# Linear attention with a mixture of experts on one core: a new beginning, two PSUM banks each for two block tiles, and a table computed in single steps

## The reference, cut to what matters

```python
x = L0_attn_x                                   # 8 x 512 x 128, float32
n = layernorm(x)                                # over the last axis
q, k, v = n @ wq.T + bq, n @ wk.T + bk, n @ wv.T + bv      # 16 heads of 8
out = ((q @ k.T) * causal) @ v                  # per head, no softmax
x = x + out @ wo.T + bo
m = layernorm(x)                                # 4096 tokens
probs = softmax(m @ Wg)                         # 8 experts
topk_p, topk_i = top_k(probs, 2)
for each token and each of its two experts e:
    y = relu(m @ W1[e] + b1[e]) @ W2[e] + b2[e] # 128 -> 256 -> 128
    x = x + topk_p * y
```

## Time and profile before

| what | us |
|---|---|
| median of 3 runs (lowest, highest) | 295.95 (294.81, 296.66) |
| the profiled execution's own time | 294.35 |
| its span in the profile | 292.6 |
| busy: PE, PEld, DVE, ACT, POOL | 242.0, 173.6, 202.1, 170.0, 180.4 |

### The profile page before, as it was taken

One profiled execution on the slowest core, in us unless ns is written; L12 is line 12 of the kernel. 1 busy time (PEld: TensorE's weight loads), 2 busy tenths in 40 slices (PEclk: granted clock), 3 DMA queues, 4 the chain that ended last, 5 costly groups with the idle time before them and its releaser, 6 DMA issues.

```text
span 292.6 us, 6373 instructions
## 1 busy us (share of the span) xinstructions
PE 242.0 (83%) x1392; PEld 173.6 (59%) x1392; DVE 202.1 (69%) x598; ACT 170.0 (58%) x675; POOL 180.4 (62%) x175
## 2 busy tenths in 40 slices
PE   0389999999999999999877196599999999989810
PEld 0134466666666666665566085487777877778600
DVE  4865999888999998999966647733344343333386
ACT  3233348888989888877696154345555555545400
POOL 3055565220877878687727777777767666666730
PEclk9999999999999999999955579979999999999965
DMA  6960000000010111010101451333444333349548
GB/s 198 307 189 0 0 3 0 0 2 2 27 39 30 39 38 38 30 46 28 58 18 55 101 143 57 87 90 112 137 119 106 96 95 92 88 101 365 164 124 262
DMA packets 32431, 25.49 MB, mean 87 GB/s; under 512 B 4337, under 2 KB 30201, under 8 KB 32396
## 3 DMA queue, kind: packets, MB, share of 16 engines
q1 hardware_dynamic: 23824, 14.52, 18.5%
q0 software_dynamic: 4320, 8.47, 8.7%
q10 hardware_dynamic: 4252, 2.10, 2.6%
HBM read 13.92 MB, written 11.61 MB: 87 GB/s over the span
## 4 chain that ended last, share of the span: by engine, by line
PE 71%; DVE 16%; issue 5%; ACT 4%; DMA 1%; ACTq 1%; DVEq 0%
PE ps L961 18%; PE ps L1060 14%; PE ps L1049 13%; PE ps L931 8%; PE ps L1042 3%; PE ps L970 2%; DVE x_sb L917 2%; PE ps L933 2%; PE ps L952 2%; PE ps L981 2%; DVE back L677 2%; DVE x_sb L915 2%; PE ps L973 1%; DVE back L668 1%; DMA bias_bc<-b_o 1%
## 5 line engine op out<-in xcount | busy, mean ns | idle before, releaser
L417 POOL DMA_INDIRECT returned<-y_sb,xt x71 | 70.9, 998 | 28.5 <-issue 25.1
L389 POOL DMA_INDIRECT dispatched<-rows,slot x64 | 65.0, 1016 | 38.0 <-ACT rows L483 16.6
L872 DVE TENSOR_SCALAR y_sb<-ps,xt 128x128 f32<-128x128 f32 x71 | 24.9, 350 | 61.1 <-PE ps L1061 61.1
L961 PE MATMUL ps<-back,causal 128*128 128x512 f32 x128 | 63.4, 618 | 0.4 <-DVE back L668 0.4
L1060 PE MATMUL ps<-w_sb,hT 128*128 x284 | 49.8, 298 | 8.4 <-DVE y_sb L872 6.8
L1049 PE MATMUL ps<-xT,w_of 128*128 128x128 f32 x284 | 49.4, 298 | 2.9 <-ACT hT L565 1.9
L373 POOL TENSOR_TENSOR back<-qkv 128x1024 f32<-128x1024 f32 x16 | 31.3, 1958 | 32.7 <-ACT qkv L504 32.4
L1060 PEld LDWEIGHTS ps<-w_sb,hT 128*128 128x128 f32 x284 | 37.6, 192 | 22.2 <-issue 22.2
L557 ACT ACTIVATE xT<-ps 128x128 f32<-128x128 f32 x71 | 19.7, 278 | 51.1 <-PE ps L1042 49.9
L565 ACT ACTIVATE hT<-ps,b_col 128x128 f32<-128x128 f32 x142 | 44.1, 366 | 1.3 <-PE ps L1049 1.3
L677 DVE TENSOR_TENSOR back<-ps,qkv 128x1024 f32<-128x1024 f32 x32 | 38.9, 1216 | 6.8 <-PE ps L961 6.8
(11 more groups left out here) (168 smaller groups left out, 416.1 us busy)
## 6 DMA issues: line engine op xcount, KB each, us to landing
xt<-dispatched SPq DMA_DIRECT2D x71, 65.0 KB, 1.9
back<-returned SPq DMA_DIRECT2D x7, 512.0 KB, 7.4
x_sb<-x SPq DMA_DIRECT2D x8, 256.0 KB, 5.2
out<-x_sb ACTq DMA_DIRECT2D x7, 256.0 KB, 2.5
returned<-y_sb,xt POOLq DMA_INDIRECT x71, 2.4
w_sb<-w SPq DMA_DIRECT2D x1, 1024.0 KB, 5.7
w_sb<-w SPq DMA_DIRECT2D x2, 512.0 KB, 7.7
dispatched<-rows,slot POOLq DMA_INDIRECT x64, 2.3
```

Of the source, the lines that this page charges most:

```text
L389: pool.indirect_dma_start(out=dispatched[:, :], out_offset=bass.IndirectOffsetOnAxis(ap=slot[:, g * K + k:g * K + k + 1], axis=0), in_=row ...
L417: pool.indirect_dma_start(out=returned[:, :], out_offset=bass.IndirectOffsetOnAxis(ap=xt[:, n % G, D:D + 1].bitcast(I32), axis=0), in_=y_s ...
L872: dve.tensor_scalar(y_sb[:, n % G, :], ps_y, xt[:, n % G, D + 1:D + 2], None, ALU.mult).then_inc(y_done, 1)
L961: mm = pe.matmul(ps_run[g % 2][:, u, :], causal[:, :], outer[:, g % OUTER_RING, 512 * u:512 * (u + 1)], start=True, stop=True)
```

## The change

1. **Biases:** the four biases come as one array, so ACT issues three loads instead of six, and DVE waits for three.
2. **Unread matmuls:** PE no longer waits for the q/k/v weights before everything. It issues nine 128x128 float32 matmuls of the identity with itself as soon as the identity is there, two more behind the first transpose, and two more between the first projection and its bias. Nothing reads them. They write bank 2.
3. **Later logarithms:** the groups are tiles 0 to 3, 4 to 11 and 12 to 31. `deviation1(1)` runs in ACT's slot 0 instead of -2, `deviation1(2)` in slot 7 instead of 1, and DVE's `scale1_out(2)` in its slot 5 instead of 0.
4. **Statistics in DVE's first slots:** ahead of the slots DVE takes the statistics of batches 0 to 3 only, and those of batches 4 to 7 at the end of its slots -1, 0, 1 and 2.
5. **Two banks each:** `ps_x` alternates between banks 2 and 0, `ps_y` between banks 5 and 6. PE's waits are for the block before the last one.
6. **Second table's steps apart:** `rest_table(k)` runs one step, or a few short ones, behind block steps 3, 5, 7, 9, 10, 11, 13, 15 and 17. No operation is dropped.

```diff
-    AHEAD = [range(0, T), range(T, 2 * T), range(2 * T, N)]
+    AHEAD = [range(0, T), range(T, 3 * T), range(3 * T, N)]
...
-        ps_x = ps[:, 2, 0:P]
+        ps_x = [ps[:, 2, 0:P], ps[:, 0, 0:P]]
         ps_h = [ps[:, 3 + u, 0:H] for u in range(2)]
-        ps_y = ps[:, 5, 0:D]
+        ps_y = [ps[:, 5 + u, 0:D] for u in range(2)]
...
             for part in range(3):
-                act.dma_start(bias_bc[32 * part:32 * part + 1, 0:3 * D], b_qkv.rearrange("(one n) -> one n", one=1)).then_inc(bias_in, 16)
-                act.dma_start(bias_bc[32 * part:32 * part + 1, 3 * D:4 * D], b_o.rearrange("(one n) -> one n", one=1)).then_inc(bias_in, 16)
+                act.dma_start(bias_bc[32 * part:32 * part + 1, :], b_qkvo.rearrange("(one n) -> one n", one=1)).then_inc(bias_in, 16)
...
-                if g == 0 or g == 3:
-                    deviation1(1 if g == 0 else 2)
+                if g == 2 or g == 9:
+                    deviation1(1 if g == 2 else 2)
...
+            def statistics_ahead(g):
+                if 1 <= g <= 4:
+                    mean1_out(g + 3)
...
             def scales_ahead(g):
-                if g == 0:
+                if g == 5:
                     scale1_out(2)
...
             mean1_out(1)
+            mean1_out(2)
             scale1_out(1)
-            for b in range(2, B):
-                mean1_out(b)
+            mean1_out(3)
...
             tile_stages = [(5, add_residual), (9, softmax_end), (1, attend_sum), (8, softmax_start), (0, attend), (0, scales_ahead),
-                           (9, places), (2, state_out), (-2, outer_product)]
+                           (9, places), (2, state_out), (-2, outer_product), (-2, statistics_ahead)]
...
+            def rest_table(k):
+                if k == 3:
+                    rest_ends()
+                elif k == 5:
+                    with nc.allow_low_precision("zero or one is exact in bfloat16"):
+                        step(dve.tensor_tensor(past[1], block_no[:, 0:REST].unsqueeze(2).to_broadcast([1, REST, QE]),
+                                               end_rest[:, :].unsqueeze(1).to_broadcast([1, REST, QE]), ALU.is_ge))
+                elif k == 7:
+                    step(dve.tensor_tensor(skipped[1], past[1], expert_step[:, :].unsqueeze(1).to_broadcast([1, REST, QE]), ALU.mult))
+                elif k == 9:
+                    step(dve.tensor_reduce(expert_f[1][:, :], skipped[1], AX_X, ALU.add))
+                elif k == 10:
+                    experts_of(1)
+                elif k == 11:
+                    step(dve.scalar_tensor_tensor(out=start_row[:, 0:QE], in0=taken[:, 0:QE], scalar=float(P), in1=region_of[:, :],
+                                                  op0=ALU.mult, op1=ALU.add))
+                    step(dve.tensor_tensor(jump[1][:, :], start_row[:, 1:QE + 1], start_row[:, 0:QE], ALU.subtract))
+                    step(dve.scalar_tensor_tensor(out=jump[1][:, :], in0=n_rest[:, :], scalar=-float(P), in1=jump[1][:, :],
+                                                  op0=ALU.mult, op1=ALU.add))
+                elif k == 13:
+                    step(dve.tensor_tensor(skipped[1], past[1], jump[1][:, :].unsqueeze(1).to_broadcast([1, REST, QE]), ALU.mult))
+                elif k == 15:
+                    step(dve.tensor_reduce(row_f[1][:, :], skipped[1], AX_X, ALU.add))
+                elif k == 17:
+                    step(dve.scalar_tensor_tensor(out=row_f[1][:, :], in0=row_f[1][:, :], scalar=start_row[:, 0:1],
+                                                  in1=block_row[:, 0:REST], op0=ALU.add, op1=ALU.add))
+                    dve.tensor_scalar(row_at[1][:, :], row_f[1][:, :], float(PAD_BLOCK), None, ALU.min).then_inc(table_done[1], 1)
...
             for k in range(-3, BLOCKS + 5):
                 block_step(block_stages, k)
-                if k == 6:
-                    rest_ends()
-                elif k == 9:
-                    rest_experts()
-                elif k == 12:
-                    rest_rows()
+                rest_table(k)
...
                 pe.transpose(ps_T1, xn[:, g % RING, :], ident[:, :]).then_inc(T1_done, 1)
+                if g == 0:
+                    unread(2)
...
+                if g == 0:
+                    pe.wait_ge(w_qkv_in, 16)
                 pe.matmul(ps_qkv, xnT[:, g % RING, :], wqkv_sb[:, :], start=True, stop=False)
+                if g == 0:
+                    unread(2)
                 wait(pe, bias_done, 4)
...
+            def unread(n):
+                for _ in range(n):
+                    pe.matmul(ps[:, 2, 0:P], ident[:, :], ident[:, :], start=True, stop=True)
...
             pe.wait_ge(ident_done, 1)
-            pe.wait_ge(w_qkv_in, 16)
+            unread(9)
...
-                wait(pe, xT_done, n)
-                pe.transpose(ps_x, xt[:, n % G, 0:D], ident[:, :]).then_inc(TX_done, 1)
+                wait(pe, xT_done, n - 1)
+                pe.transpose(ps_x[n % 2], xt[:, n % G, 0:D], ident[:, :]).then_inc(TX_done, 1)
...
-                wait(pe, y_done, n)
+                wait(pe, y_done, n - 1)
                 for c in range(HC):
-                    pe.matmul(ps_y, hT[:, n % W, c, :], w2_sb[:, c, bass.ds(w2_from[n], D)], start=(c == 0), stop=False)
+                    pe.matmul(ps_y[n % 2], hT[:, n % W, c, :], w2_sb[:, c, bass.ds(w2_from[n], D)], start=(c == 0), stop=False)
```

More of the change, by code:

```diff
@@ L34, in tile_slots, with preln_linear_attention_moe @@
                 stage(s - lag)
-def preln_linear_attention_moe(nc, x, w_qkv, b_qkv, w_o, b_o, w_gate, w1, b1, w2, b2, out):
+def preln_linear_attention_moe(nc, x, w_qkv, b_qkvo, w_o, w_gate, w1, b1, w2, b2, out):
     B, L, D = x.shape
@@ L556, in xT_out @@
                 wait(act, h_mm, n + 1 - W)
-                act.activation(xT[:, n % W, :], ps_x, ACT.Identity).then_inc(xT_done, 1)
+                act.activation(xT[:, n % W, :], ps_x[n % 2], ACT.Identity).then_inc(xT_done, 1)
             def hT_out(n):
@@ L813, in first_table @@
                 experts_of(0)
-                rows_from(0, FIRST, E)
+                step(dve.tensor_tensor(skipped[0], past[0], jump[0][:, :].unsqueeze(1).to_broadcast([1, FIRST, E]), ALU.mult))
+                step(dve.tensor_reduce(row_f[0][:, :], skipped[0], AX_X, ALU.add))
                 step(dve.tensor_tensor(row_f[0][:, :], row_f[0][:, :], block_row[:, 0:FIRST], ALU.add))
@@ L834, in rest_ends @@
                 step(dve.tensor_tensor_scan(end_rest[:, :], one_row[:, :], n_rest[:, :], 0.0, ALU.mult, ALU.add))
-            def rest_experts():
-                with nc.allow_low_precision("zero or one is exact in bfloat16"):
-                    step(dve.tensor_tensor(past[1], block_no[:, 0:REST].unsqueeze(2).to_broadcast([1, REST, QE]),
-                                           end_rest[:, :].unsqueeze(1).to_broadcast([1, REST, QE]), ALU.is_ge))
-                step(dve.tensor_tensor(skipped[1], past[1], expert_step[:, :].unsqueeze(1).to_broadcast([1, REST, QE]), ALU.mult))
-                step(dve.tensor_reduce(expert_f[1][:, :], skipped[1], AX_X, ALU.add))
-                experts_of(1)
@@ L1057, in output @@
                 wait(pe, hT_done, HC * (n + 1))
-                wait(pe, y_done, n)
+                wait(pe, y_done, n - 1)
                 for c in range(HC):
-                    pe.matmul(ps_y, hT[:, n % W, c, :], w2_sb[:, c, bass.ds(w2_from[n], D)], start=(c == 0), stop=False)
-                pe.matmul(ps_y, ones[:, :], b2_parts[:, bass.ds(w2_from[n], D)], start=False, stop=True).then_inc(y_mm, 1)
+                    pe.matmul(ps_y[n % 2], hT[:, n % W, c, :], w2_sb[:, c, bass.ds(w2_from[n], D)], start=(c == 0), stop=False)
+                pe.matmul(ps_y[n % 2], ones[:, :], b2_parts[:, bass.ds(w2_from[n], D)], start=False, stop=True).then_inc(y_mm, 1)
             block_stages = [(2, hidden), (0, transpose_x), (4, output), (-3, registers)]
```

20 lines of the change are left out of this document (3 added, 17 removed).

## The result

The changed kernel takes 279.97 us (median of 4 runs, 278.9 to 280.82) beside 295.84 for the kernel before (4 runs, 294.81 to 296.66): a ratio of 0.946, with a 95% interval of 0.942 to 0.951, so faster by 5.4%. Its profiled execution took 280.46 with a span of 278.7. The prediction was 282.1, with a range of 278.0 to 289.0.

What follows compares the result with a forecast made beforehand. Most of the chain was taken as PE's, with something else behind it in three stretches. Gains of 6.5 (beginning, slots) and 7.3 (blocks, end), 13.8 together, take 294.35 to 280.55; 1.6 more gives 282.1 us, range 278.0 to 289.0.

Steps and rivals of the forecast that it cites:

- the median of the runs shown is 1.6 above the profiled one: Whole kernel: last step, from a predicted execution of 280.55 to a predicted median of 282.1.
- They cost nothing: Beginning: nine unread matmuls run while the bias split is awaited anyway; without that cover up to 5.
- three batches now stand behind `attend(0)`: 7.9 - 3.1 = 4.8: First attention slots: three batches of statistics on full DVE take 3.1 of the 7.9 lead, leaving 4.8.
- POOL does that at another time now: up to 1.5 more: Attention slots: DVE's outer product of 2.71 no longer meets POOL's bias split; up to 1.5 more, 6.3.
- The chosen 6.5: Beginning and attention slots: gain taken between ends of 4.8 and 7.9, nearest to DVE's sum.
- Both gaps go: Blocks: with the second table's steps apart, PE's two stops, 2.82 and about 2.5, disappear.
- 70 starts at 1.32 are 92.4, plus 0.5: Blocks: POOL's returns set the pace from 182.58; last return at 275.5 against 280.32, 4.8 gained.
- The tail: End, behind the last return: landing 2.9, fetch 3.4, additions 0.84, then 2.25; 9.8 instead of 12.3, 2.5 gained.
- A: Beginning: the clock does not hold, PE stays at half rate; loss 4.7, time 286.8; chance 0.20.
- B: Block 32: PE restarts at half clock after its stop and POOL starves for results; time 285; chance 0.11.
- C: Blocks: DVE's weight copies lock POOL out, a return takes 1.57; slower, time 299; chance 0.04.
- D: Blocks: the second bank buys no rate, 1.39 being PE's own; time 283.3; chance included in the forecast's 0.60.

Runs made afterwards that it cites:

- e2: The changed kernel with the statistics of batches 4 to 7 ahead of DVE's slots again, as before the change; 279.03 us, ratio 0.946.
- e4: The changed kernel with the second table's steps in three lumps again, behind block steps 6, 9 and 12, two banks kept; 277.93 us, ratio 0.944.
- e3: The changed kernel with one bank each for `ps_x` and `ps_y` and the earlier waits again; 285.54 us, ratio 0.973.
- e9: The changed kernel with statistics, later logarithms and second scale back where the kernel before has them; 283.70 us, ratio 0.960.
- e5: The changed kernel with one more unread 128-column matmul in each of the 71 blocks; 281.71 us, ratio 0.956.
- e1: The changed kernel without its thirteen unread matmuls; 284.38 us, ratio 0.966.

## Why the prediction was right, and where it was not

**The sum** was 13.8 in the profiled execution and came out at 13.9; the 2.1 between 282.1 and 279.97 is the step "the median of the runs shown is 1.6 above the profiled one". It is the offset of one execution of before, and I carried it over; the changed kernel's profiled execution was 0.5 above its own median. Within the 13.9 three terms were off and cancelled.

**Biases, unread matmuls, later logarithms.** The first bias was done at 9.1 (9.5 predicted), `deviation1(1)` ended at 11.5 (12.0), the running sums started at 14.94 (15.5) and `attend(0)` at 16.86 (17.4). Each term is good to half a microsecond, all in one direction, from a bias landing at 5.96 instead of 6.2 and a split that followed it. "They cost nothing" held. What the steps did not say is that the unread matmuls and the later logarithms are each worth little alone.

**Statistics in slots.** The step "three batches now stand behind `attend(0)`: 7.9 - 3.1 = 4.8" failed. Of the lead of 8.4 only 1.1 was lost by `attend(3)`, not 3.1, and e2, which has the statistics before the slots, ends up no more than 0.6 better (6.6 against 6.0). The step beside it, "POOL does that at another time now: up to 1.5 more", failed too. The collision moved from DVE's second outer product to its fourth, and from POOL's first subtraction to its second, and grew, from 2.71 to 3.13. The chosen 6.5 was close to the 6.0 measured at the last `attend` for neither reason: 8.4, less 1.1 in the first slots, less 2.1 at the collision, plus 0.8 at `attend(9)`.

**From the last `attend` to the first return** the sum had no term. It lost 0.2, net: dispatches began earlier still (6.85), since they no longer waited for ACT's rows but for DVE's slots, and lost 1.05 in 24 dispatches beside the table's operations.

**Second table apart.** "Both gaps go" was right and worth nothing here: e4. PE's gaps were on the path of before, and are beside the store of after.

**Two banks.** The block was 1.11 and the end by POOL, as said. The term "70 starts at 1.32 are 92.4, plus 0.5" came out at 91.5: the 1.32 had long ones of before in it, and the steady pitch is 1.29. That gives 6.3 instead of 4.8. The tail was taken at 9.8 and took 10.45: 3.31 to land the last return, where I took 2.9, 2.84 for the fetch instead of 3.4, and 1.68 for the additions, where I took 0.84. Two parts, not one, wait for the last rows, and their four additions stand behind each other. Both together 8.1 for 7.3. By e3 5.4 to 6.3 of it are the second banks' own.

**The rivals.** A fell, but e9 has shown the state it describes: projections of 1.65 at a granted clock of 0.50, with 4.5 lost where A had 4.7. And it fell with some luck: in two of eleven traces with this beginning the clock did fall, for 3.4 us, at a cost of some 1.2 in e5, a size between forecast and A that the prediction did not have. B fell by 0.05 us of store; a chance of 0.11 was too small for so thin a margin, though e5 suggests that the price beyond it is gentle. C fell at 1.307 a return. D fell with e3: the second bank does buy the rate, and without it the time is 285.5, not 283.3, as POOL runs out of store and the additions queue up behind the last result.

**Open:** what spreading the table is worth with one bank; what decides whether the clock falls at 13.6 in this beginning; and single waits of POOL of 1.5 in e3.

## What to carry to other kernels

When an engine far down the chain runs at its own rate, write down for every step how much work lies in store for it: an edit before it pays only where that store is empty, and the store says how near the next bound is. Test edits of one stretch in pairs, since a gap that one leaves can undo what another bought: the unread matmuls are worth 5 us with the logarithm out of the way, and 1.7 at most with it in the way, in the execution that was profiled. When a stretch is moved in time, look again at what now runs beside it on DVE and POOL.

## What the runs showed of the hardware

- **An operation of DVE with both inputs in SBUF and an operation of POOL that reads SBUF exclude each other**, and the one that starts second stands until the first has ended: 3.13 against 1.21 (DVE second), 2.98 against 2.12 (POOL second). The Trainium skill ("SBUF — State Buffer", "SBUF: two separate sides") calls the ports that the two share an exclusive lock that goes to whichever starts first; these rows agree to within 0.15 us. POOL's operation need not have two inputs. In the changed kernel a cast of POOL with one, 1.04 in the kernel before (at 33.82), takes 2.06 (timelines of DVE and POOL):

```profile
29.21 1.21 DVE L671 TENSOR_TENSOR back<-qkv 128x1024 f32<-128x1024 f32 x1
29.25 2.06 POOL L403 CAST b_middle<-b_bc 128x1024 bf16<-128x1024 f32 x1
```

- **The issue of a dispatch on POOL is held up in the same way by DVE's operations with two SBUF inputs, even on one partition**: 1.58 and 1.77 beside steps of 1.12. Earlier in the changed kernel four dispatches beside DVE's outer products take 1.29 to 1.68. A reduction of the same 936 numbers (1.11), with one input, leaves a dispatch at 0.95, and so does the same multiplication with one small input in PSUM (0.96). The float32 copies of weights, from which the prediction made rival C, fall once in every block and leave the returns at 0.98 to 1.1. So in this kernel the two inputs hold a dispatch, and a cost of copies within SBUF cannot be seen.
- **A granted clock of 1.00 in the first microseconds of these profiles is no measurement.** In e1 the window from 10 to 15 shows 1.00 with projections of 1.65:

```profile
10.00:15.00 5.00, 4.17 (x8) 1.57 (x8) 4.34 (x24) 2.16 (x8) 2.09 (x5) 1.00 1.15 319
```

  The trace of e1 has its first record of the clock at 20.5, and the first projection of 0.81 starts at 20.59; ahead of the first record the row stands at 1.00 for want of one. In e9 the records begin at 5.1, and its row for the same window shows 0.50. So in the first microseconds the durations tell the rate.
- **An unread 128x128 float32 matmul costs 0.22 at the full rate**, as two records 0.11 apart, in a stream of blocks (1.11 to some 1.34) as in a run of its own. At half rate the records of the nine stand 0.21 apart.
